# Scores two units ahead placed in front of the attention product in every unit of a pair loop

## The reference

```python
x = x + 0.5 * _L0_ffn_ref(_layernorm(x), A, B, Wr)
x = x + _L0_attn_ref(_layernorm(x), wq, wkv, wo)
x = x + 0.5 * _L0_ffn_ref(_layernorm(x), A, B, Wr)

# attention, per batch of 256 tokens and head (DN = DV = 128)
scores = jnp.einsum('bqhd,bkhd->bhqk', q[..., :DN], k) * scale
scores = jnp.where(causal[None, None], scores, NEG_INF)
probs = jax.nn.softmax(scores, axis=-1)
attn = jnp.einsum('bhqk,bkhd->bqhd', probs, v).reshape(B, S, H * DV)
return jnp.einsum('bse,ed->bsd', attn, wo)

# experts: top 16 of 64 by x @ Wr.T, softmax over them, rank 16 each
out = jnp.einsum('nkr,kdr->nd', (x @ A) * gates, B) * 2.0
```

## Time and profile before

| | us |
|---|---|
| median of three timed executions | 1036.54 (1036.46 to 1036.55) |
| the profiled execution, device time | 1036.7 |
| its span, first to last instruction | 1034.7 |
| TensorE busy | 1023.6 (99%) |
| VectorE busy | 687.5 (66%) |
| ScalarE busy | 554.0 (54%) |
| GpSimd busy | 533.4 (52%) |

### The profile page before, as it was taken

One profiled execution on the slowest core, in us unless ns is written; L12 is line 12 of the kernel. 1 busy time (PEld: TensorE's weight loads), 2 busy tenths in 40 slices (PEclk: granted clock), 3 DMA queues, 4 the chain that ended last, 5 costly groups with the idle time before them and its releaser, 6 DMA issues.

```text
span 1034.7 us, 18708 instructions
## 1 busy us (share of the span) xinstructions
PE 1023.6 (99%) x5588; PEld 888.9 (86%) x5588; DVE 687.5 (66%) x1815; ACT 554.0 (54%) x1480; POOL 533.4 (52%) x473
## 2 busy tenths in 40 slices
PE   8999999999999999999999999999999999999998
PEld 7999888888888888888888888888878888889997
DVE  6778852432467766767776766776787988766553
ACT  4112455555367676667666667666776566531110
POOL 5431378996189777779777788777420000000000
PEclk9999999999999999999999999999999999999999
DMA  9700254772734444453444444443568878840000
GB/s 365 321 0 1 82 203 183 264 265 93 254 92 134 146 144 127 152 155 140 138 145 133 144 158 145 133 148 130 168 251 322 310 240 291 288 159 11 21 20 31
DMA packets 83704, 168.17 MB, mean 163 GB/s; under 512 B 8528, under 2 KB 24912, under 8 KB 82640
## 3 DMA queue, kind: packets, MB, share of 16 engines
q1 hardware_dynamic: 83664, 167.68, 47.2%
HBM read 102.37 MB, written 63.44 MB: 160 GB/s over the span
## 4 chain that ended last, share of the span: by engine, by line
PE 94%; DVE 3%; ACT 1%; POOL 1%; DMA 1%; issue 0%; POOLq 0%
PE bank L276 28%; PE bank L278 28%; PE bank L277 27%; PE bank L565 4%; PE bank L554 3%; PE bank L583 3%; PE bank L332 1%; PE bank L284 1%; DMA o_raw<-keep_o 0%; PE bank L359 0%; POOL wq_lo L1329 0%; PE bank L542 0%; DVE prob L1103 0%; DMA x<-x_in 0%; DVE upT_lo L1953 0%
## 5 line engine op out<-in xcount | busy, mean ns | idle before, releaser
L1320 POOL TENSOR_SCALAR ve<-mv 128x1 f32<-128x1 f32 x24 | 6.3, 264 | 306.6 <-DVE mv L976 306.3
L680 ACT ACTIVATE bank<-bank,nmax 128x128 f32<-128x128 f32 (+1 forms) x256 | 105.6, 453 | 4.4 <-DVE nmax L1090 4.4
L1103 DVE TENSOR_SCALAR prob<-bank,rinv 128x128 f32<-128x128 f32 (+1 forms) x256 | 95.1, 414 | 4.6
L276 PE MATMUL bank<-xc_lo,wq_hi 128*128 128x512 f32 x224 | 91.7, 410 | 0.4 <-POOL wq_lo L1329 0.4
L1090 DVE CUSTOM_DVE_ANT_0 bank<-bank,mask 128x128 f32<-128x128 f32 (+1 forms) x256 | 83.5, 389 | 11.4 <-PE bank L278 11.4
L276 PE MATMUL bank<-o_lo,ow_hi 128*128 128x512 f32 x224 | 88.9, 397 | 2.1 <-DVE o_lo L969 2.1
L634 ACT CAST o_hi<-o_raw 128x1024 fp32r<-128x1024 f32 x56 | 59.2, 1057 | 55.1 <-DMA o_raw<-keep_o 48.4
L276 PE MATMUL bank<-xc_lo,wk_hi 128*128 128x512 f32 x224 | 88.7, 396 | 0.0
L278 PE MATMUL bank<-xc_hi,wq_hi 128*128 128x512 f32 x224 | 87.9, 393 | 0.0
L278 PE MATMUL bank<-xc_hi,wk_hi 128*128 128x512 f32 x224 | 87.6, 391 | 0.0
L278 PE MATMUL bank<-o_hi,ow_hi 128*128 128x512 f32 x224 | 87.4, 390 | 0.0
(11 more groups left out here) (168 smaller groups left out, 3148.7 us busy)
## 6 DMA issues: line engine op xcount, KB each, us to landing
o_raw<-keep_o SPq DMA_DIRECT2D x49, 512.0 KB, 4.3
keep_v<-out_hl SPq DMA_DIRECT2D x64, 256.0 KB, 2.3
v<-keep_v SPq DMA_DIRECT2D x64, 256.0 KB, 3.5
keep_o<-att_comb SPq DMA_DIRECT2D x60, 256.0 KB, 2.3
keep_o<-att SPq DMA_DIRECT2D x45, 256.0 KB, 3.1
stage_v<-wv SPq DMA_DIRECT2D x4, 2048.0 KB, 9.1
stage_wq<-wqk SPq DMA_DIRECT2D x16, 512.0 KB, 3.3
keep_vraw<-out_raw SPq DMA_DIRECT2D x64, 128.0 KB, 2.1
```

The costliest lines, as they stand in the source:

```text
L276: nc.tensor.matmul(dst, a_hi, b_lo, start=first, stop=False, skip_group_check=onto)
L680: nc.scalar.activation(sp[b][:, a:e], sp[b][:, a:e], ACT.Exp, bias=nmax[:, c:c + 1], scale=-1.0, accum_out=rsum[:, c:c + 1]).then_inc(s["e ...
L1103: nc.vector.tensor_scalar(prob[:, b, a:e], sp[b][:, a:e], rinv[:, c:c + 1], None, ALU.mult).then_inc(s["p_ready"], 1)
```

## The change

In each unit steps 4 and 5 change places: the scores two units ahead now come directly behind the wait for `pT_split`, and the attention product behind the scores.

```diff
@@ -610,11 +610,11 @@
                 if first and j == 0:
                     pe_scores(pe, 0, 1)
                 pe.wait_ge(s["pT_split"], 2 * u + 2)
-                pe_attend(pe, p, j)
                 if j < 2:
                     pe_scores(pe, p, j + 2)
                 elif not final:
                     pe_scores(pe, p + 1, j - 2)
+                pe_attend(pe, p, j)
                 if final:
```

## The result

The changed kernel takes 1038.18 us (median of 20 executions, 1037.48 to 1040.73) against 1036.62 for the kernel before (20 executions, 1036.07 to 1038.36). The ratio is 1.0015, with a 95% interval of 1.0009 to 1.0021: 1.6 us slower, less than the 0.2% that the prediction called telling, but clear of the noise of twenty executions. The predicted 1036.2 is 2.0 us low, and the time lies 0.3 us above the range. The later comparisons of the same kernel gave 1.0015 again (1038.36 against 1036.86).

The account below looks back on a forecast made before the run. The prediction took TensorE's product stream to bound the kernel. From the median of 1036.54 us, terms of -0.3 + 0 + 0 + 0 gave 1036.2 us, with a range of 1035.0 to 1037.9.

Parts of the forecast that it names:

- What bounds the kernel: Pair loop: TensorE, 99% busy with no listed waits in the looped pairs, lasts as long as its products stream.
- Term 1, the stream: TensorE, attention start to second 512-column start: 2.54 us against 2.55 in 62 units; -0.6 us, half taken, -0.3.
- Term 2, operands sooner: Scores need q and k parts 1.15 us sooner; margins of 0.90 us or more cover it; 0 us.
- Term 3, attention's result later: Attention ends 1.16 us later; ScalarE's copy, GpSimd's combination and SyncE's transfers absorb it; 0 us.
- Term 4, scores sooner: Scores come 1.15 us sooner; VectorE's 0.82 us wait goes, but TensorE doesn't wait for what follows; 0 us.
- Rival 1, late release: At j = 3, the score block after pT_lo's release costs one weight load more, 1.7 us, time 1037.9; chance 0.10.
- Rival 2, attention's head: Attention's opening waits and register arithmetic exposed behind a short product, up to 0.08 us a unit, time 1041.2; chance 0.06.
- Rival 3, faster: Sooner scores release something TensorE waits for; moved blocks touch 0.4 us; time 1034.3; chance 0.04.
- no change by 0.2%: Whole kernel: time stays within 0.2%, 2.1 us, of the kernel before; chance 0.90.

Follow-up runs that it names:

- the plain product third: Changed kernel with attention's plain two-pass product moved between its second and third rounded products, against the kernel before: 1037.58 us, ratio 1.0008.
- the plain product first: Changed kernel with attention's plain two-pass product moved ahead of its three rounded ones, against the kernel before: 1036.59 us, ratio 0.9997.

## Why the prediction missed

**What bounds the kernel:** right. TensorE's stream sets the time of the loop, and no wait was added in it. One detail was misread: of the two waits for pT_lo one, 0.22 us at 755.28, lies in the fourteenth looped pair. It costs nothing more in the new order.

**Term 1, the stream: the step that failed.** The pieces were right, and so was their sum, 2.54 against 2.55 us. Wrong was where the sum ended, at the second wide start: the stream behind it was put at no difference, without a reason. It isn't the same: in unit 1 the eleven starts that follow take 2.54 instead of 2.50. Per pair, from the table, the four units take 31.26 instead of 31.15 us (first traces) or 31.28 instead of 31.13 (second), 0.11 to 0.14; times 15.5 pairs that is 1.7 to 2.2 us, against 1.55 and 1.99 read from the loops without the unit in which the wait for o_lo scatters. The term was put at -0.3 and measured about +1.6. The rows would have shown it. The wide products behind the transposes, a few places ahead of those quoted, stood at 235, 228 and 232 ns in the trace of before, and the attention block that I took as a model in the last pair is followed by starts at 0.24, 0.23 and 0.24; I read two rows behind it and stopped. The uncertainty that I gave to the term, 1.2 us, was that of rounding, not of a model cut off too early, and this is why the range missed.

**Term 2, operands sooner:** right. No wait for q or k parts appears on TensorE. In the changed kernel's unit 3, kT_lo on VectorE runs from 504.99 and ends 0.9 us ahead of the scores' start at 506.59, as before; pT_lo ends at 506.35.

```profile
504.99 0.69 DVE L969 TENSOR_TENSOR kT_lo<-bank,kT_hi 128x512 fp32r<-128x512 f32 x1 [0.93 <-ACT kT_hi L634]
505.60 0.75 DVE L969 TENSOR_TENSOR pT_lo<-bank,pT_hi 128x256 fp32r<-128x256 f32 x2
```

**Term 3, attention's result later:** right, with the size a little off. ScalarE, the answer to the earlier trace rows, in order of time:

```profile
509.10 0.59 ACT L634 COPY att<-bank 128x512 f32<-128x512 f32 x1 [0.28 <-PE bank L583]
510.48 0.37 ACT L634 COPY kT_raw<-bank 128x256 f32<-128x256 f32 x1 [0.80 <-PE bank L278]
```

The copy now waits for attention, 0.28 us, and ends 0.79 ahead of kT_raw (0.7 was forecast), which still waits for TensorE. On GpSimd the wait at wq_hi shrank by about what the combination of attention blocks waits longer: from 49.4 to 36.9 us in all between 290 and 700 us, against 11.0 to 24.8. These are the two entries in the changed kernel's list of waits for 290 to 700 us:

```profile
POOL wq_hi L1327 <- PE bank L278: 36.9, 13, 2.9
...
POOL att_comb L1336 <- ACT att L634: 24.8, 12, 2.1
```

Each wait at wq_hi is now at most 2.9 us where the earlier trace rows has 3.91.

**Term 4, scores sooner:** right. VectorE's maximum of j = 2 no longer waits, and the idle time stands in front of its next step, a sum that hangs on a k product which didn't move:

```profile
500.59 0.29 DVE L1090 CUSTOM_DVE_ANT_0 bank<-bank,mask 128x128 f32<-128x128 f32 x1
...
503.36 0.70 DVE L1122 TENSOR_TENSOR bank<-bank,s 128x512 f32<-128x512 f32 x1 [1.41 <-PE bank L278]
```

**Rival 1, late release:** didn't happen. The first score product starts 0.23 after the last wide one. With it falls the use made of the Trainium skill ("TensorE: Matmul & The Clock Gate", section "Wait — 56ns, not 53.3ns?"): a sequencer's 62 ns per matmul as a price after each late release. No such gap is in the trace, whichever decode was on. Where the release really comes late, in the last unit of the fourteenth pair, the unit takes 7.52 and 7.51 us in the two traces, and 7.59 in both of the kernel before.

**Rival 2, attention's head:** didn't happen either, by the 0.12 at that seam and by the run that took the waits away from it (1038.36). Its sign was right by accident.

**Rival 3, faster:** no. Of the chances, "no change by 0.2%" was right, at 0.15%, but by luck: the 1.6 us that came are under that limit, and the term that was to bring them about had the other sign.

**What stays open:** why the wide products run at 235, 233, 236, 224, 231, 236, 228, 232, 231 ns before they settle at 227. Most slow stretches are pieces of this one sequence: the changed kernel enters at its first number, the transposes mostly at about the fourth (224, 231, 236, 228), the plain product third at 233, the plain product first at 232, the kernel before behind its end. That reads like a state that is set at one moment and that wide products work off one step each; this is a picture and not shown. The runs do show that the order of kinds in the last short products decides in units 1 and 2 how many slow starts follow.

Short products are not the only thing that starts the sequence. In unit 0 of the kernel before, in its second trace, the first seven wide products behind the block start 226 to 227 ns apart and the next ones 236, 231, 236, 229 and 232, on average over 13 pairs; slow starts are there in all 13, and in 9 of 13 in the first trace. The seventh one's weight load, the last row below, starts 0.09 us behind the sixth product (516.53 against 516.44), where the next loads start within 0.01 of the product before. The rows are from the second trace, the last one in order of time on the weight loads, the others on TensorE:

```profile
516.44 0.39 PE L278 MATMUL bank<-xc_hi,wq_hi 128*128 128x512 f32 x1
516.66 0.40 PE L276 MATMUL bank<-xc_lo,wq_hi 128*128 128x512 f32 x1
516.90 0.39 PE L277 MATMUL bank<-xc_hi,wq_lo 128*128 128x512 f32 x1
517.13 0.40 PE L278 MATMUL bank<-xc_hi,wq_hi 128*128 128x512 f32 x1
...
516.53 0.19 PEld L276 LDWEIGHTS bank<-xc_lo,wq_hi 128*128 128x128 f32 x1
```

Behind a block that ends in a two-pass product the weight load of the second wide product is late as well, by 0.08 us (524.51, where the first one starts at 524.43, in the changed kernel). Whether a late weight load is the common cause, no run tests, and in the first trace four pairs have the load 0.07 late and no slow start. Which part of the chip holds the state, no trace tells.

## What to carry to other kernels

On an engine that is never idle, the order of products counts even where no wait changes, if only a little (here 1.6 us of 1037): end a run of short products with the kind after which the long ones run at full pace, and look at their starts until they are back at their steady distance. A sum over a seam has to reach that far on both sides; a model piece from elsewhere in the trace is to be read to its end, not to its second row. And a difference of 20 to 40 ns in a unit is the whole result when there are 62 units: means over many repetitions tell it, single rows at 0.01 us don't.

## What was not expected of the hardware

A rounded 128x512 product starts 227 ns after the one before it in the steady stream, and 224 to 236 ns for nine starts behind a run of short products that ends in a two-pass one, 43 ns in all beyond the 0.08 us by which the first one's successor is late. What stood ahead of a block of six transposes can be felt behind it (unit 0 slower by 0.023 us with only units 2 and 3 changed). In one program, with the same products, behind unit 3's block of the kernel before the slow starts are there in 8 of 13 pairs of the first trace and in all of the second, and behind the transposes of unit 1 the first has the longer slow stretch, six starts against two. The units of its two traces differ by up to 0.02 us each and a pair by 0.017, which is 0.25 us over the loop for this alone.
